# Layer 3 of a four-layer kernel: weighing the gathered rows and the Hadamard transform of z, done in other places

## The chip, the cores and the metric

The kernel runs on one core of one Trainium2 chip. The metric is the device time of one execution in microseconds (us). The runs of the kernel before took 1693.89, 1694.31 and 1697.46 us; the median is 1694.31.

## The reference, cut to what matters

Four layers run behind one another on x, 4 x 512 tokens of 512 channels. Each makes a `ratio` (a scan over time, times a gate of x) and sends it through a feed-forward part. Layer 2 is a mixture of 8 experts with the 2 best taken; its output y is, for each token, the sum of two experts' rows, each times a weight of its own, and is added to x. Layer 3 is the one that the change touches:

```
x = x + y                                       # y: end of layer 2
z = ratio3 * sigmoid(x)
h = fwht(z * SU_ug)                             # Walsh-Hadamard over 512 channels
gate, up = h @ W_gate.T * s_g, h @ W_up.T * s_u # 2048 hidden channels each
hid = silu(gate) * up
x = x + (fwht(hid * SU_dp) @ W_down.T) * s_d
```

A transform over 512 = 4 x 128 channels is a product of a transform over the 4 blocks of 128 channels and one over the 128 channels in each block. The 128-channel part is a matrix (H128) that can be applied to z or, since it is symmetric, to the weights that z is multiplied with. The factors 1/sqrt(n) lie in the scales.

## The kernel before, in words

Channels lie on partitions, tokens along the free dimension. Layer 3 is cut into 4 batches (`BATCH`) of 512 tokens (`TIME`) and 8 chunks (`NCHUNK`) of 256 hidden channels, so 32 units i, chunk by chunk, 4 batches in each. A unit is four products of gate and up (`product`, L2514, 12 matmuls of 512 columns each) and one `down` (L2533, 24 matmuls). Every operand is split into a high part rounded to fp32r and the low rest, and a product is three matmuls: high x high, low x high, high x low. Units 0 to 3 are the first chunk and belong to the start of the layer, in which each batch's z is also made; units 4 to 31 are one steady loop. `gate_up(i)` is followed by `down(i-1)`, so that the work on the hidden channels lies beside TensorE.

For batch i, in order: GpSimd gathers, for each of 4 tiles of 128 tokens, two rows of expert output for each token (`gather`, L1584); VectorE makes diagonal matrices of the weights (`diagonals`, L1592); TensorE turns and weighs with them in one, 32 fp32 matmuls (`cols_of_y`, L1601); `gated` on VectorE adds to x (`residual`, L1647), multiplies with the gate and the ratio (`z`, L1655) and takes the low part (`z_low`, L1660), while ScalarE makes the sigmoid (L1623) and the high part (L1627). Then TensorE transforms all four 128-channel blocks (`fwht`, L1614, 32 matmuls with H128 or its negative), and ScalarE and VectorE split the result again (L1640, L1680). The four blocks of z have one buffer each, `g[0..3]`. `cols_of_y` and `fwht` write the same four PSUM banks as `down`, `p_o`.

The order on each engine is written out by hand (L2445 to L2473 for ScalarE, L2542 to L2575 for TensorE, L2622 to L2647 for VectorE); each engine works through its list in order and waits on semaphores. On the hidden channels ScalarE computes `silu` (L2436) and `high_h` (L2443), VectorE `hidden` (L2593), GpSimd `low_h` (L2487), VectorE `add` (L2603). up of unit i may start when `hidden` of unit i-1 has read the same bank (the event `h0` or `h1`), gate when `silu` has. Weights of a chunk are loaded by SyncE into one buffer `raw`, split by ScalarE (`high`, L2426) and GpSimd (`low`, L2481; chunk 0 by VectorE, `first_low`, L2609), two chunks in turn. Sigmoid and silu live in different ScalarE tables, so going from one to the other costs a table load.

Of the kernel before, what the change touches and what calls it, by code (L numbers as in the profile page):

```python
# [15 lines left out]
P = 128  # L16
# [6 lines left out]
UNITS = CT * BATCH  # L23
FF0, FF1, FF3 = 2048, 1024, 2048
# [1488 lines left out]
class LayerStart:  # L1513
# [3 lines left out]
    def __init__(self, core, scope, d, up_front):  # L1517
# [7 lines left out]
        self.minus_H = sb("in3_minus_H", [P, P], F32R)  # L1525
        self.diag = [[sb(f"in3_diag{k}_{t}", [P, P]) for t in range(TPB)] for k in range(2)]
# [14 lines left out]
class LayerInput:  # L1541
# [4 lines left out]
    def __init__(self, core, scope, c, d, ratio, banks, spare, start):  # L1546
# [7 lines left out]
        self.minus_H, self.su, self.diag = start.minus_H, start.su_ug, start.diag  # L1554
# [31 lines left out]
    def diagonals(self, eng, i):  # L1586
        if i >= 1:
            eng.wait_ge(*self.E("cols_of_y").at(CT * (i - 1) + CT - 1))
        for t in range(TPB):
            for k in range(2):  # L1590
                weight = self.c["moe_weight"][:, i * TPB + t, k:k + 1]
                last = eng.tensor_scalar(self.diag[k][t][:, :], self.c["ident"][:, :], weight, None, ALU.mult)  # L1592
        last.then_inc(*self.E("diag").inc)

    def cols_of_y(self, eng, i):
        eng.wait_ge(*self.E("diag").at(i))
        for t in range(TPB):
            eng.wait_ge(*self.gathered[i % 2 * TPB + t].at(i // 2 * 2 + 1))
            for o in range(CT):
                for k in range(2):  # L1600
                    last = eng.matmul(self.banks[:, o, t * P:(t + 1) * P], self.parts[i % 2][k][t][:, o * P:(o + 1) * P],  # L1601
                                      self.diag[k][t][:, :], start=k == 0, stop=k == 1)
                if t == TPB - 1:
                    last.then_inc(*self.E("cols_of_y").inc)

    def fwht(self, eng, i):
        eng.wait_ge(*self.E("minus_H").at(0))
        eng.wait_ge(*self.E("x").at(CT * i + CT - 1))
        for k in range(CT):
            eng.wait_ge(*self.E("z_low").at(CT * i + k))  # L1610
            for j in range(CT):
                h = self.minus_H if (k & j).bit_count() % 2 else self.c["H128"]
                for t, part in enumerate((self.high(i), self.low(i))):
                    last = eng.matmul(self.banks[:, j, :], h[:, :], part[:, k, :],  # L1614
                                      start=(k + t == 0), stop=(k == CT - 1 and t == 1))
                if k == CT - 1:
                    last.then_inc(*self.E("fwht").inc)
# [7 lines left out]
    def z_high(self, eng, n):  # L1625
        eng.wait_ge(*self.E("z").at(n))
        eng.activation(self.high(n // CT)[:, n % CT, :], self.g[n % CT][:, :], ACT.Copy).then_inc(*self.E("z_high").inc)  # L1627

    def gate_and_round(self, eng, i):
        n = CT * i  # L1630
        self.gate(eng, n)
        for k in range(CT):
            if k + 1 < CT:
                self.gate(eng, n + k + 1)
            self.z_high(eng, n + k)

    def round_transformed(self, eng, i):
        for j in range(CT):
            eng.wait_ge(*self.E("fwht").at(CT * i + j))
            eng.activation(self.high(i)[:, j, :], self.banks[:, j, :], ACT.Copy).then_inc(*self.E("high").inc)  # L1640

    def constants(self, eng):
        eng.tensor_scalar(self.minus_H[:, :], self.c["H128"][:, :].bitcast(F32), -1.0, None, ALU.mult).then_inc(*self.E("minus_H").inc)
# [13 lines left out]
    def z_low(self, eng, n):  # L1657
        k, g = n % CT, self.g[n % CT][:, :]
        eng.wait_ge(*self.E("z_high").at(n))
        eng.tensor_tensor(self.low(n // CT)[:, k, :], g, self.high(n // CT)[:, k, :].bitcast(F32), ALU.subtract).then_inc(*self.E("z_low").inc)  # L1660

    def gated(self, eng, i):
# [6 lines left out]
        self.z_low(eng, n)  # L1669
        self.residual(eng, n + 3)  # L1670
        self.z(eng, n + 2)
        self.z_low(eng, n + 1)
        self.z(eng, n + 3)
        self.z_low(eng, n + 2)
        self.z_low(eng, n + 3)

    def low_transformed(self, eng, i):
        for j in range(CT):
            eng.wait_ge(*self.E("high").at(CT * i + j))
            eng.tensor_tensor(self.low(i)[:, j, :], self.banks[:, j, :], self.high(i)[:, j, :].bitcast(F32), ALU.subtract).then_inc(*self.E("low").inc)  # L1680
# [673 lines left out]
def gated_ffn(core, c, d, ratio, block, before, start):  # L2354
# [10 lines left out]
    w_hi, w_lo = E("weights_hi"), E("weights_lo")  # L2365
    with ExitStack() as s:
# [11 lines left out]
        p_o = core.banks(s, "ffn3_po", [P, CT, TIME])  # L2378
        inp = LayerInput(core, s, c, d, ratio, p_o, (wh[1], wl[1]), start)
# [396 lines left out]
```

## Time and profile before

| | before |
|---|---|
| median of 3 runs | 1694.31 us |
| the profiled execution's own time | 1693.09 us |
| its span | 1691.3 us |
| TensorE busy | 1481.3 us, 88% |
| VectorE busy | 1123.0 us, 66% |
| ScalarE busy | 969.2 us, 57% |
| GpSimd busy | 468.3 us, 28% |
| granted TensorE clock, mean | 0.96 |

The span runs from the first to the last instruction; the execution's own time is a little longer. PE is TensorE (PEld its weight load), DVE VectorE, ACT ScalarE, POOL GpSimd, SP SyncE (SPq its queue). Matmuls are pipelined, so the length of one is longer than the distance between two starts; the distances are what adds up. fp32 matmuls leave two records each, transposes one.

### The profile page before, as it was taken

To read this page: it belongs to the slowest core of one execution; us is meant where nothing else is said; L and a number is where in the kernel's file an instruction comes from. 1 tells how busy PE (TensorE), PEld (TensorE's weight loads), DVE (VectorE), ACT (ScalarE), POOL (GpSimd) and SP (SyncE) were. 2 spreads that over 40 slices of the span, in tenths; PEclk is the share of its full clock that TensorE was granted. 3 is DMA by queue.
4 is the path that set the end of the run, shared out by engine and by line. 5 is a ranking of instruction groups with operands and counts; after the bars stand their busy time and mean duration, and the time that the engine had idled before them with its cause. 6 is when DMAs were issued, how large, how long until landed. Compare 5 with 4: busy or idle time off the path is not lost.

```text
span 1691.3 us, 19555 instructions
## 1 busy us (share of the span) xinstructions
PE 1481.3 (88%) x6389; PEld 959.4 (57%) x6422; DVE 1123.0 (66%) x1718; ACT 969.2 (57%) x1270; POOL 468.3 (28%) x434
## 2 busy tenths in 40 slices
PE   5666579999975699996599999699999999999999
PEld 2222234444432456665544444378788888888887
DVE  6899589999996799995777778754422223222223
ACT  5766499999984799995266877543321221221111
POOL 0000133644431222220044545550231321322211
PEclk9999799999997899999699999899999999999999
DMA  7756642221115898875654545570110100101002
GB/s 279 274 203 209 232 155 76 63 82 63 63 44 152 233 232 211 210 165 193 257 160 148 170 154 168 193 254 1 38 38 1 38 25 14 38 0 38 1 13 88
DMA packets 105495, 210.37 MB, mean 124 GB/s; under 512 B 11508, under 2 KB 28404, under 8 KB 101684
## 3 DMA queue, kind: packets, MB, share of 16 engines
q1 hardware_dynamic: 90500, 173.72, 29.9%
q0 software_dynamic: 14896, 35.40, 9.6%
q8 instruction: 54, 0.88, 0.2%
q14 instruction: 45, 0.37, 0.1%
HBM read 140.13 MB, written 52.17 MB: 114 GB/s over the span
## 4 chain that ended last, share of the span: by engine, by line
PE 49%; DMA 2%; DVE 2%; ACT 1%; issue 0%; POOL 0%; SPq 0%; POOLq 0%; DVEq 0%; ACTq 0%
PE ffn_po L2533 10%; PE ffn_pu L2514 10%; PE ffn_pg L2514 10%; PE moe_psum L1920 8%; PE moe_psum L1941 4%; PE ffn_po L1614 2%; PE ffn_po L1601 1%; PE moe_psum L1859 1%; PE moe_psum L1908 1%; DMA rows_of_z<-moe_zrow 1%; PE moe_psum L1931 0%; DMA in_part<-expert_out,moe_source 0%; DVE x L1647 0%; DVE up_front L1655 0%; DMA rt_consts<-in_route 0%
## 5 line engine op out<-in xcount | busy, mean ns | idle before, releaser
L2593 DVE SCALAR_TENSOR_TENSOR up_front<-ffn_pu,ffn_up_scale,up_front 128x512 f32<-128x512 f32 x64 | 48.0, 751 | 289.9 <-PE ffn_pu L2514 289.9
L2436 ACT ACTIVATE up_front<-ffn_pg,ffn_gate_chunk 128x512 f32<-128x512 f32 x64 | 44.1, 689 | 320.7 <-PE ffn_pg L2514 320.7
L2487 POOL TENSOR_TENSOR ffn_hl<-up_front,ffn_hh 128x512 fp32r<-128x512 f32 x64 | 82.9, 1296 | 396.2 <-ACT ffn_hh L2443 396.2
L2603 DVE SCALAR_TENSOR_TENSOR x<-ffn_po,ffn_out_scale,x 128x512 f32<-128x512 f32 x128 | 95.6, 750 | 75.1 <-PE ffn_po L2533 75.1
L2514 PE MATMUL ffn_pg<-zhi,ffn_wh 128*128 128x512 f32 x256 | 101.5, 397 | 0.5
L2533 PE MATMUL ffn_po<-ffn_hh,ffn_wh 128*128 128x512 f32 x256 | 100.6, 393 | 1.3 <-DVE x L1647 1.3
L2514 PE MATMUL ffn_pu<-zhi,ffn_wh 128*128 128x512 f32 x256 | 100.9, 394 | 0.0
L2514 PE MATMUL ffn_pg<-zhi,ffn_wl 128*128 128x512 f32 x256 | 100.4, 392 | 0.0
L2514 PE MATMUL ffn_pu<-zhi,ffn_wl 128*128 128x512 f32 x256 | 100.4, 392 | 0.0
L2533 PE MATMUL ffn_po<-ffn_hh,ffn_wl 128*128 128x512 f32 x256 | 100.1, 391 | 0.0
L2514 PE MATMUL ffn_pg<-zlo,ffn_wh 128*128 128x512 f32 x256 | 99.6, 389 | 0.0
L2533 PE MATMUL ffn_po<-ffn_hl,ffn_wh 128*128 128x512 f32 x256 | 99.6, 389 | 0.0
L2514 PE MATMUL ffn_pu<-zlo,ffn_wh 128*128 128x512 f32 x256 | 99.3, 388 | 0.0
L965 POOL TENSOR_SCALAR l_rr<-l_ss 128x1 f32<-128x1 f32 x32 | 16.9, 529 | 268.0 <-ACT l_junk L877 203.9
L2443 ACT ACTIVATE ffn_hh<-up_front 128x512 fp32r<-128x512 f32 x64 | 40.2, 628 | 86.5 <-DVE up_front L2593 86.5
L1920 PE MATMUL moe_psum<-up_front,moe_zc 128*128 x156 | 75.1, 605 | 0.0
L1941 PE MATMUL moe_psum<-moe_down,moe_hc 128*128 x156 | 72.2, 593 | 1.9 <-ACT moe_hc L2050 1.9
L1920 PE MATMUL moe_psum<-moe_up_back,moe_zc 128*128 x156 | 73.4, 592 | 0.0
L325 POOL TENSOR_TENSOR wkv_k<-wkv_eu,wkv_k 128x512 f32<-128x512 f32 x32 | 51.9, 1622 | 76.3 <-ACT wkv_eu L315 76.3
L1207 PE MATMUL l_pz<-H_layer,l_gate 128*128 128x512 f32 x128 | 59.8, 611 | 10.6 <-DVE l_gate L1392 10.6
L2132 POOL DMA_INDIRECT moe_zt<-rows_of_z,rt_token_list x39 | 39.9, 1022 | 102.4 <-DVE rt_token_list L2241 80.5
L1234 PE MATMUL l_pg<-H_layer,l_hh 128*128 128x512 f32 x128 | 54.2, 423 | 13.4 <-DVE l_hl L1451 12.9
(354 smaller groups left out, 4053.2 us busy)
## 6 DMA issues: line engine op xcount, KB each, us to landing
wkv_k<-in_fside SPq DMA_DIRECT2D x64, 256.0 KB, 4.3
ratio<-wkv_fn SPq DMA_DIRECT2D x64, 256.0 KB, 3.3
wkv_ek<-exp_k SPq DMA_DIRECT2D x48, 256.0 KB, 3.0
wkv_ekv<-exp_k_times_v SPq DMA_DIRECT2D x48, 256.0 KB, 3.7
expert_out<-moe_eo SPq DMA_DIRECT2D x39, 256.0 KB, 2.2
up_front<-in_gated SPq DMA_DIRECT2D x8, 1024.0 KB, 4.9
x<-in_x SPq DMA_DIRECT2D x4, 1024.0 KB, 7.4
down_first_a<-in_down_raw SPq DMA_DIRECT2D x16, 256.0 KB, 2.6
```

What stands on the lines that cost most here:

```text
L325: eng.tensor_tensor(self.k[p][:, :], self.eu[p][:, :], self.k[p][:, :], ALU.mult).then_inc(*self.E("euv").inc)
L1207: last = eng.matmul(p_z[:, :], z[p][:, k * P:(k + 1) * P], hadamard_row(k).bitcast(F32), start=k == 0, stop=k == CT - 1)
L1234: last = eng.matmul(p_g[:, m * 512:(m + 1) * 512], part[p][:, m * 512 + k * P:m * 512 + (k + 1) * P], hadamard_row(k), start=(k + t == 0), ...
L1920: last = eng.matmul(p_gu[j % 2][:, :], zc[j % ZCS][:, k * P:(k + 1) * P], up[k][:, ds(columns[j], WCOL)], start=k == 0, stop=k == CT - 1)
L1941: last = eng.matmul(p_eo[j % 2][:, :], hc[j % 2][:, k * P:(k + 1) * P], down_w[:, ds(columns[j] + k * EXPERTS * CH, CH)], start=k == 0, st ...
L2436: eng.activation(hf[t], p_g[t][:, :], ACT.Silu, scale=scale).then_inc(*E(f"silu{t}").inc)
L2443: eng.activation(hh[t][slot % 2][:, :], hf[t], ACT.Copy).then_inc(*E(f"hh{t}").inc)
L2487: eng.tensor_tensor(hl[t][slot % 2][:, :], hf[t], hh[t][slot % 2][:, :].bitcast(F32), ALU.subtract).then_inc(*E(f"hl{t}").inc)
L2514: last = eng.matmul(ps[:, :], chunk_w(part, slot, which, k, t), z[:, k, tok], start=(n == 0), stop=(n == 3 * CT - 1))
L2533: last = eng.matmul(p_o[:, o, :], chunk_w(w, slot, "down", k, o), h[k][slot % 2][:, :], start=(n == 0), stop=(n == 3 * HT - 1))
L2593: eng.scalar_tensor_tensor(hf[t], p_u[t][:, :], scale, hf[t], ALU.mult, ALU.mult).then_inc(*E(f"h{t}").inc)
L2603: eng.scalar_tensor_tensor(x[:, o, :], p_o[:, o, :], out_s[:, o:o + 1], x[:, o, :], ALU.mult, ALU.add).then_inc(*E("x").inc)
```

## The change

1. Rows are weighed before they are turned. ScalarE multiplies the first expert's row by its weight (`weigh_first`), VectorE multiplies the second's and adds (`weigh_second`), TensorE only transposes (`cols_of_y`, 16 transposes). `diagonals` and the negative of H128 go. For odd batches the weighed rows lie in the weights' buffer `raw`, so the load of chunk 1 waits until the last batch's rows are turned.
2. The 4-block part of the transform is done by VectorE as butterflies on the four buffers of z: `inner` (blocks 0 and 1, 2 and 3), then `outer` (across the pairs). The blocks are finished in the order 2, 0, 3, 1 (`AS_MADE`), and the products go through them in this order. The high part is taken behind the butterflies, once. `fwht`, `round_transformed` and `low_transformed` go.
3. The 128-channel part is applied to the gate and up weights of each chunk: `turn_weights`, 8 matmuls with H128 in 4 pieces of 512 columns, into the banks of gate and up; ScalarE and VectorE split the result back into the weight buffers (`high_turned`, `low_turned`). For chunks 2 to 7 this stands at the unit with i mod 4 = 2, a unit and a half ahead of use, three pieces in front of `down` and one behind; for chunk 1 between down(2) and down(3), which is moved ahead of gate_up(4); for chunk 0 ahead of everything.
4. The orders on TensorE, ScalarE and VectorE are written anew. In batches 0 to 3 `hidden` stands behind the next-but-one batch's `weigh_second`, and `next_cols` waits for x alone.

Where a function is rewritten, only its new lines are shown; the old ones stand above.

```diff
+AS_MADE = (2, 0, 3, 1)
...
-        self.minus_H = sb("in3_minus_H", [P, P], F32R)
-        self.diag = [[sb(f"in3_diag{k}_{t}", [P, P]) for t in range(TPB)] for k in range(2)]
+        self.spare = sb("in3_spare", [P, TIME])[:, :]
...
+        self.y = [start.parts, [start.raw[:, t * CH:(t + 1) * CH] for t in range(TPB)]]
...
-                eng.wait_ge(*self.E("cols_of_y").at(CT * (i - 2) + CT - 1))
+                eng.wait_ge(*(self.E("y").at(TPB * (i - 2) + t) if i % 2 else self.E("cols_of_y").at(CT * (i - 2) + CT - 1)))
...
+    def weigh_first(self, eng, i, raw_read):
         for t in range(TPB):
             eng.wait_ge(*self.gathered[i % 2 * TPB + t].at(i // 2 * 2 + 1))
+            if i % 2 and t == 0:
+                eng.wait_ge(*(raw_read.at(0) if i == 1 else self.E("cols_of_y").at(CT * (i - 2) + CT - 1)))
+            eng.activation(self.y[i % 2][t], self.parts[i % 2][0][t], ACT.Identity,
+                           scale=self.c["moe_weight"][:, i * TPB + t, 0:1]).then_inc(*self.E("first").inc)
+    def weigh_second(self, eng, i):
+        for t in range(TPB):
+            eng.wait_ge(*self.gathered[i % 2 * TPB + t].at(i // 2 * 2 + 1))
+            eng.wait_ge(*self.E("first").at(i * TPB + t))
+            y, second = self.y[i % 2][t], self.parts[i % 2][1][t]
+            eng.scalar_tensor_tensor(y, second, self.c["moe_weight"][:, i * TPB + t, 1:2], y,
+                                     ALU.mult, ALU.add).then_inc(*self.E("y").inc)
+    def cols_of_y(self, eng, i):
+        for t in range(TPB):
+            eng.wait_ge(*self.E("y").at(i * TPB + t))
             for o in range(CT):
+                last = eng.transpose(self.banks[:, o, t * P:(t + 1) * P], self.y[i % 2][t][:, o * P:(o + 1) * P],
+                                     self.c["ident"][:, :])
                 if t == TPB - 1:
                     last.then_inc(*self.E("cols_of_y").inc)
...
-            eng.wait_ge(*self.E("z_low").at(n - CT))
+            eng.wait_ge(*self.E("z_low").at(n // CT * CT - 1))
...
+    def gates(self, eng, i):
         for k in range(CT):
+            self.gate(eng, CT * i + k)
+    def z_high(self, eng, i):
+        for m, k in enumerate(AS_MADE):
+            eng.wait_ge(*self.E("outer").at(CT * i + m))
+            eng.activation(self.high(i)[:, k, :], self.transformed(k), ACT.Copy).then_inc(*self.E("z_high").inc)
...
+    def inner(self, eng, i, pair):
+        eng.wait_ge(*self.E("z").at(CT * i + 2 * pair + 1))
+        if pair:
+            eng.wait_ge(*self.E("inner").at(CT * i + 1))
+        even, odd = (self.g[2 * pair + k][:, :] for k in range(2))
+        apart = self.g[1] if pair else self.spare
+        eng.tensor_tensor(apart, even, odd, ALU.subtract).then_inc(*self.E("inner").inc)
+        eng.tensor_tensor(even, even, odd, ALU.add).then_inc(*self.E("inner").inc)
+    def transformed(self, k):
+        return self.g[(0, 1, 3, 2)[k]][:, :]
+    def outer(self, eng, i):
+        eng.wait_ge(*self.E("inner").at(CT * i + CT - 1))
+        g = [t[:, :] for t in self.g]
+        eng.tensor_tensor(g[3], g[0], g[2], ALU.subtract).then_inc(*self.E("outer").inc)
+        eng.tensor_tensor(g[0], g[0], g[2], ALU.add).then_inc(*self.E("outer").inc)
+        eng.wait_ge(*self.E("outer").at(CT * i + 1))
+        eng.tensor_tensor(g[2], self.spare, g[1], ALU.subtract).then_inc(*self.E("outer").inc)
+        eng.tensor_tensor(g[1], self.spare, g[1], ALU.add).then_inc(*self.E("outer").inc)
+    def z_low(self, eng, i):
+        for m, k in enumerate(AS_MADE):
+            eng.wait_ge(*self.E("z_high").at(CT * i + m))
+            eng.tensor_tensor(self.low(i)[:, k, :], self.transformed(k), self.high(i)[:, k, :].bitcast(F32),
+                              ALU.subtract).then_inc(*self.E("z_low").inc)
...
         self.residual(eng, n + 2)
         self.z(eng, n + 1)
         self.residual(eng, n + 3)
         self.z(eng, n + 2)
+        self.inner(eng, i, 0)
         self.z(eng, n + 3)
+        self.inner(eng, i, 1)
+        self.outer(eng, i)
+        self.z_low(eng, i)
...
+    PIECES = 2 * GU // TIME
+    turned, turned_hi, turned_lo = E("weights_turned"), E("turned_hi"), E("turned_lo")
...
+        p_w = [p_g[0], p_u[0], p_g[1], p_u[1]]
+        piece = lambda t, n: t[:, n * TIME:(n + 1) * TIME]
...
+                if i == BATCH:
+                    eng.wait_ge(*inp.E("cols_of_y").at(UNITS - 1))
...
+            def high_turned(m):
+                for n in range(PIECES):
+                    eng.wait_ge(*turned.at(PIECES * m + n))
+                    eng.activation(piece(wh[m % 2], n), p_w[n][:, :], ACT.Copy).then_inc(*turned_hi.inc)
...
             high(0, 0)
+            high_turned(0)
+            inp.weigh_first(eng, 0, w_lo)
+            inp.gates(eng, 0)
+            inp.z_high(eng, 0)
+            inp.weigh_first(eng, 1, w_lo)
+            for i in range(1, BATCH):
+                inp.gates(eng, i)
+                for t in range(HT):
+                    silu(i - 1, i - 1, t)
+                inp.z_high(eng, i)
+                if i + 1 < BATCH:
+                    inp.weigh_first(eng, i + 1, w_lo)
+                for t in range(HT):
+                    high_h(i - 1, i - 1, t)
             high(BATCH, BATCH)
+            for i in range(BATCH - 1, N):
                 for t in range(HT):
                     silu(i, i % U, t)
                 for t in range(HT):
                     high_h(i, i % U, t)
+                if i == BATCH - 1:
+                    high_turned(1)
                 if i % BATCH == 1 and i + 3 < N:
                     high(i + 3, (i + 3) % U)
+                if i % BATCH == 2 and i + 2 < N:
+                    high_turned((i + 2) // BATCH)
...
-                eng.wait_ge(*w_lo.at(i // BATCH))
+                eng.wait_ge(*turned_lo.at(PIECES * (i // BATCH) + PIECES - 1))
+                if i % BATCH == 3 and i >= BATCH and i + 1 < N:
+                    eng.wait_ge(*turned_lo.at(PIECES * (i // BATCH + 1) + p_w.index(ps)))
                 if i >= 1:
                     eng.wait_ge(*E(free).at(i - 1))
                 n = 0
-                for k in range(CT):
+                for m, k in enumerate(AS_MADE):
                     if i < BATCH:
-                        eng.wait_ge(*inp.E("low").at(CT * i + k))
+                        eng.wait_ge(*inp.E("z_low").at(CT * i + m))
...
+                eng.wait_ge(*w_lo.at(i // BATCH))
...
+            def turn_weights(m, i, pieces):
+                eng.wait_ge(*w_lo.at(m))
+                for n in pieces:
+                    if i is not None:
+                        eng.wait_ge(*E(("silu", "h")[n % 2] + str(n // 2)).at(i))
+                    for t, part in enumerate((wh, wl)):
+                        last = eng.matmul(p_w[n][:, :], c["H128"][:, :], piece(part[m % 2], n), start=t == 0, stop=t == 1)
+                    last.then_inc(*turned.inc)
             def next_cols(i):
 
+                eng.wait_ge(*inp.E("x").at(CT * i - 1))
                 inp.cols_of_y(eng, i)
 
             before(eng, "zc", "h", "hc", "eo")
+            turn_weights(0, None, range(PIECES))
             inp.cols_of_y(eng, 0)
             product(0, 0, "gate", 0)
+            next_cols(1)
             product(0, 0, "up", 0)
             product(0, 0, "gate", 1)
             product(0, 0, "up", 1)
             product(1, 1, "gate", 0)
+            next_cols(2)
             product(1, 1, "up", 0)
             product(1, 1, "gate", 1)
+            product(1, 1, "up", 1)
             eng.wait_ge(*inp.E("x").at(CT * 2 + CT - 1))
             down(0, 0)
             product(2, 2, "gate", 0)
             product(2, 2, "up", 0)
+            eng.wait_ge(*E("x").at(CT * 0 + CT - 1))
             next_cols(3)
             product(2, 2, "gate", 1)
+            product(2, 2, "up", 1)
             eng.wait_ge(*inp.E("x").at(CT * 3 + CT - 1))
             down(1, 1)
             for i in range(3, N + 1):
                 if i < N:
                     gate_up(i, i % U)
+                m = (i + 2) // BATCH if i % BATCH == 2 and i + 2 < N else None
+                if m is not None:
+                    turn_weights(m, i, range(PIECES - 1))
+                if i != BATCH:
+                    down(i - 1, (i - 1) % U)
+                if m is not None:
+                    turn_weights(m, i, range(PIECES - 1, PIECES))
+                if i == BATCH - 1:
+                    turn_weights(1, i, range(PIECES))
+                    down(i, i)
...
+            def low_turned(m, pieces):
+                for n in pieces:
+                    eng.wait_ge(*turned_hi.at(PIECES * m + n))
+                    eng.tensor_tensor(piece(wl[m % 2], n), p_w[n][:, :], piece(wh[m % 2], n).bitcast(F32),
+                                      ALU.subtract).then_inc(*turned_lo.inc)
             first_low()
+            low_turned(0, range(PIECES))
+            inp.weigh_second(eng, 0)
             inp.gated(eng, 0)
+            inp.weigh_second(eng, 1)
+            for i in range(1, BATCH):
+                inp.gated(eng, i)
+                if i >= 2:
+                    add(i - 2, i - 2)
+                if i + 1 < BATCH:
+                    inp.weigh_second(eng, i + 1)
+                for t in range(HT):
+                    hidden(i - 1, i - 1, t)
+            for i in range(BATCH - 1, N + 1):
                 if i < N:
                     if i % BATCH == 0:
                         chunk_scale(i, i % U)
                     for t in range(HT):
                         hidden(i, i % U, t)
+                m = (i + 2) // BATCH if i % BATCH == 2 and i + 2 < N else None
+                if m is not None:
+                    low_turned(m, range(PIECES - 1))
+                if i != BATCH:
+                    add(i - 1, (i - 1) % U)
+                if m is not None:
+                    low_turned(m, range(PIECES - 1, PIECES))
+                if i == BATCH - 1:
+                    low_turned(1, range(PIECES))
+                    add(i, i)
```

## Rows read from the trace of the kernel before

**Rows 1.** The chain of waits, 1087 to 1225 us: start us, length us, what
```profile
1103.84 9.24 PE ffn_po L1614 x32
...
1118.93 7.14 PE ffn_po L1601 x64
...
1131.59 7.44 PE ffn_po L1614 x32
...
1203.88 3.00 PE ffn_pg L2514 x12
1206.88 2.75 PE ffn_pu L2514 x12
...
1215.12 5.49 PE ffn_po L2533 x24
```

**Rows 2.** The same chain later: in the steady loop, and its last piece
```profile
1253.60 2.76 PE ffn_pg L2514 x12
...
1676.93 10.94 PE ffn_po L2533 x48
```

**Rows 3.** Busy time of each engine by stretch: a batch, then the steady loop
```profile
1178.00:1210.00 32.00, 31.23 (x165) 26.08 (x164) 14.07 (x23) 14.81 (x19) 5.34 (x3) 1.00 0.00 1
...
1309.00:1440.00 131.00, 131.00 (x574) 107.36 (x573) 35.81 (x50) 25.55 (x34) 34.45 (x18) 1.00 0.07 25
```

**Rows 4.** TensorE's timeline: four transposes in the experts and what follows
```profile
1060.52 0.60 PE L1908 MATMUL moe_psum<-ident,moe_zt 128*128 128x128 f32 x4
1060.96 1.88 PE L1920 MATMUL moe_psum<-up_front,moe_zc 128*128 x4
```

**Rows 5.** VectorE's timeline: first weight split, batch 0's first instructions
```profile
1087.62 3.37 DVE L2609 TENSOR_TENSOR ffn_wl<-up_front,ffn_wh 128x3072 fp32r<-128x3072 f32 x1
...
1099.06 1.28 DVE L1647 TENSOR_TENSOR x<-x,ffn_po 128x512 f32<-128x512 f32 x2 [8.07 <-PE ffn_po L1601]
1100.53 0.75 DVE L1655 SCALAR_TENSOR_TENSOR up_front<-up_front,in_su,zhi 128x512 f32<-128x512 f32 x1 [0.18 <-ACT up_front L1623]
1101.19 0.68 DVE L1647 TENSOR_TENSOR x<-x,ffn_po 128x512 f32<-128x512 f32 x1
1101.79 0.74 DVE L1655 SCALAR_TENSOR_TENSOR up_front<-up_front,in_su,zhi 128x512 f32<-128x512 f32 x1
1102.45 0.68 DVE L1660 TENSOR_TENSOR zlo<-up_front,zhi 128x512 fp32r<-128x512 f32 x1
```

**Rows 6.** ScalarE's timeline: four copies, a rounding, a table load
```profile
1111.72 2.07 ACT L1640 ACTIVATE zhi<-ffn_po 128x512 fp32r<-128x512 f32 x4 [5.40 <-PE ffn_po L1614]
...
1119.76 0.63 ACT L2443 ACTIVATE ffn_hh<-up_front 128x512 fp32r<-128x512 f32 x1 [2.85 <-DVE up_front L2593]
1120.41 1.28 ACT L1623 ACT_TABLE_LOAD   x1
```

**Rows 7.** TensorE's timeline behind idle time (in brackets), earlier layer first
```profile
576.52 0.50 PE L1234 MATMUL l_pg<-H_layer,l_hh 128*128 128x512 f32 x1 [2.85 <-DVE l_hl L1451]
576.86 0.40 PE L1234 MATMUL l_pg<-H_layer,l_hl 128*128 128x512 f32 x1
...
1103.84 0.58 PE L1614 MATMUL ffn_po<-zhi,H 128*128 128x512 f32 x1 [3.47 <-DVE x L1647]
1104.21 0.63 PE L1614 MATMUL ffn_po<-zlo,H 128*128 128x512 f32 x1
1104.64 0.63 PE L1614 MATMUL ffn_po<-zhi,H 128*128 128x512 f32 x1
```

**Rows 8.** SyncE's queue, then DMA issues of 1080 to 1141 with landing time
```profile
1098.34 0.37 SPq L1576 DMA_DIRECT2D zhi<-ratio  x1
...
up_front<-down_full SPq DMA_DIRECT2D x1, 512.0 KB, 9.2
```

**Rows 9.** VectorE's timeline: four adds of down's result
```profile
1160.21 2.72 DVE L2603 SCALAR_TENSOR_TENSOR x<-ffn_po,ffn_out_scale,x 128x512 f32<-128x512 f32 x4
```

**Rows 10.** GpSimd's timeline: low parts of hidden channels, of a weight chunk
```profile
1136.58 2.57 POOL L2487 TENSOR_TENSOR ffn_hl<-up_front,ffn_hh 128x512 fp32r<-128x512 f32 x2
...
1252.30 6.85 POOL L2481 TENSOR_TENSOR ffn_wl<-up_front,ffn_wh 128x3072 fp32r<-128x3072 f32 x1 [1.36 <-ACT ffn_wh L2426]
```

**Rows 11.** Timelines of GpSimd, then VectorE, in the experts' last steps
```profile
1079.94 1.63 POOL L369 TENSOR_TENSOR wkv_fn<-wkv_fn,wkv_bn 128x512 f32<-128x512 f32 x1 [1.76 <-DVE wkv_bn L355]
...
1080.48 1.63 DVE L513 SCALAR_TENSOR_TENSOR wkv_fd<-wkv_fd,wkv_eu 128x512 f32<-128x512 f32 x1
...
1083.68 0.69 DVE L513 SCALAR_TENSOR_TENSOR wkv_fd<-wkv_fd,wkv_eu 128x512 f32<-128x512 f32 x1
```

More of the change, by code:

```diff
@@ L1553, in __init__ @@
         self.e = {}
-        self.minus_H, self.su, self.diag = start.minus_H, start.su_ug, start.diag
+        self.su, self.spare = start.su_ug, start.spare
         own = [start.parts, [core.sb(scope, f"in3_part{t}", [P, CH], F32)[:, :] for t in range(TPB)]]
@@ L1584, in gather @@
                 eng.indirect_dma_start(self.parts[i % 2][k][t], None, self.d["expert_out"], at).then_inc(*self.gathered[i % 2 * TPB + t].inc)
[L1586 to L1593, printed above, removed]
@@ L1599, in cols_of_y @@
             for o in range(CT):
-                for k in range(2):
-                    last = eng.matmul(self.banks[:, o, t * P:(t + 1) * P], self.parts[i % 2][k][t][:, o * P:(o + 1) * P],
-                                      self.diag[k][t][:, :], start=k == 0, stop=k == 1)
+                last = eng.transpose(self.banks[:, o, t * P:(t + 1) * P], self.y[i % 2][t][:, o * P:(o + 1) * P],
+                                     self.c["ident"][:, :])
                 if t == TPB - 1:
                     last.then_inc(*self.E("cols_of_y").inc)
-    def fwht(self, eng, i):
-        eng.wait_ge(*self.E("minus_H").at(0))
-        eng.wait_ge(*self.E("x").at(CT * i + CT - 1))
-        for k in range(CT):
[L1610 to L1617, printed above, removed]
@@ L1668, in gated @@
         self.z(eng, n + 1)
-        self.z_low(eng, n)
         self.residual(eng, n + 3)
         self.z(eng, n + 2)
-        self.z_low(eng, n + 1)
+        self.inner(eng, i, 0)
         self.z(eng, n + 3)
[L1674 to L1680, printed above, removed]
+        self.inner(eng, i, 1)
+        self.outer(eng, i)
+        self.z_low(eng, i)
 def experts(core, c, d, ratio, ratio3, up_front, up_in, block, start):
@@ L2572, in _ @@
                     gate_up(i, i % U)
-                if i == 3:
-                    eng.wait_ge(*inp.E("low").at(UNITS - 1))
-                down(i - 1, (i - 1) % U)
+                m = (i + 2) // BATCH if i % BATCH == 2 and i + 2 < N else None
[8 more added lines that the diff above has]
+                    down(i, i)
         @block.vector
         def _(eng):
-            inp.constants(eng)
             eng.wait_ge(*consts.at(3))
@@ L2620, in _ @@
             chunk_scale(0, 0)
+            def low_turned(m, pieces):
[3 more added lines that the diff above has]
+                                      ALU.subtract).then_inc(*turned_lo.inc)
             first_low()
+            low_turned(0, range(PIECES))
+            inp.weigh_second(eng, 0)
             inp.gated(eng, 0)
-            inp.diagonals(eng, 1)
-            inp.low_transformed(eng, 0)
-            hidden(0, 0, 0)
-            inp.gated(eng, 1)
-            inp.diagonals(eng, 2)
-            hidden(0, 0, 1)
-            inp.low_transformed(eng, 1)
-            hidden(1, 1, 0)
-            inp.gated(eng, 2)
-            inp.diagonals(eng, 3)
-            add(0, 0)
-            hidden(1, 1, 1)
-            inp.low_transformed(eng, 2)
-            hidden(2, 2, 0)
-            inp.gated(eng, 3)
-            add(1, 1)
-            hidden(2, 2, 1)
-            inp.low_transformed(eng, 3)
-            for i in range(3, N + 1):
+            inp.weigh_second(eng, 1)
[8 more added lines that the diff above has]
+            for i in range(BATCH - 1, N + 1):
                 if i < N:
@@ L2646, in _ @@
                         hidden(i, i % U, t)
-                add(i - 1, (i - 1) % U)
+                m = (i + 2) // BATCH if i % BATCH == 2 and i + 2 < N else None
[8 more added lines that the diff above has]
+                    add(i, i)
 def build(nc, d, out):
```

55 lines of the change are left out of this document (removed).

## The prediction, on record before the changed kernel ran

> **What bounds the kernel now.** I read the chain of waits first. From 1087 us on it is TensorE nearly alone [rows 1]: gathered rows turned and weighed (L1601), the transform of z (L1614), the products (L2514, L2533). The last product ends at 1676.93 + 10.94 = 1687.87 us [rows 2]. Then the engines' busy time by stretch [rows 3]: over one batch of the start of layer 3 (1178 to 1210) TensorE is busy 31.2 of 32 us, VectorE 14.1, ScalarE 14.8; in the long stretch behind, TensorE is busy all the time and VectorE 27% of it. So a TensorE instruction removed from this layer shortens the end by its whole length, until VectorE or ScalarE becomes late in its place. The reader should keep two prices: 12 products take 2.75 us, so 0.229 us each; 32 transform matmuls take 7.44 us, so 0.2325 each [rows 1].
>
> **The sum of TensorE's work.** Removed: `fwht`, 32 matmuls a batch, 7.44 us in batches 1 to 3 and 9.24 in batch 0, where the clock starts low [rows 1]. `cols_of_y` takes 7.14 us a batch with 32 fp32 matmuls (64 records) [rows 1]; after the change it is 16 transposes. Four transposes of the same shape in the experts take 1060.96 - 1060.52 = 0.44 us [rows 4], so 16 take 1.8 us: 5.3 us less a batch. Added: `turn_weights`, 8 matmuls of the transform's form for each of 8 weight chunks, 1.86 us a chunk. Alone this would give, from batch 1 on, 3 x (7.44 + 5.3) - 7 x 1.86 = 38.3 - 13.0 = 25.3 us. But the transform's other half is now on VectorE, and the batches' start must be walked through.
>
> **The unit of the walk: `gated` on VectorE.** Its instructions start 0.60 us (tensor_tensor) or 0.66 us (scalar_tensor_tensor) behind one another [rows 5]: `x` at 1101.19, `z` at 1101.79, next at 1102.45. Before, its z part took 12 instructions a batch, plus 4 for the rounding of the transformed. Now it is 20: 4 residuals, 4 z, 8 sums and differences, 4 roundings. The first z starts 1.47 us behind the first residual, since ScalarE's sigmoid lies between (1099.06 to 1100.53) [rows 5]. From there: the last z at +5.88; the second inner pair waits until that z has landed, +6.69; `outer` waits likewise, +8.03, and for its own first two, +9.36; the four roundings at +10.57 to +12.4. ScalarE's four copies lie one step ahead (0.52 us apart [rows 6]). Sum: **13.05 us from the first residual to the end of `gated`**, and a product can begin at +11.25, when the first rounded bank is there. With 0.1 us less or more at each of five same-engine waits I bound it at 12.5 and 13.6.
>
> **Batch 0: nothing gained.** The 8 `in_diag` instructions ahead of `first_low` go (1.7 us); it ended at 1087.62 + 3.37 = 1090.99 [rows 5] and now ends near 1089.3. Turning chunk 0 costs 8 matmuls at the low clock, 0.43 us each [rows 7], then copies and differences: done by 1094.1. All of this is covered, because the last of the first gathers lands only at 1098.3, when the queue that waits for it issues its next load [rows 8]; if that cover went, it would cost 4 us at most. Behind the landing now stand a ScalarE pass (0.63), a VectorE pass (0.75) and a transpose at low clock (0.6 with latency): first residual at 1100.35, against 1099.06. `gated` ends at 1113.4. The product waits idle for 11 us, and the clock falls: behind 3.47 us of idleness the matmuls are 0.43 us apart [rows 7]. Eight at 0.43 and four at 0.23 from 1111.65 on end at 1116.0. Before, the same product ended at 1116.2 (1113.19 + 3.0). Even.
>
> **Batch 1.** `weigh_second` (4 x 0.66) ends at 1116.1, transposes start at 1116.0, first residual at 1117.65, `gated` ends at T1 = 1130.7.
>
> **Batch 2.** VectorE: `weigh_second` +2.65, two `hidden` to +4.0. ScalarE: `high_h` 0.63, then a table load of 1.28 [rows 6], then the sigmoid; the first z starts at T1 + 6.7, 1.1 us later than VectorE alone would. T2 = T1 + 18.3 = 1149.0. TensorE has 8.25 + 5.5 us to do in it beside its 2.75: covered.
>
> **Batch 3.** Here a new wait decides. TensorE's order is product(2, gate), product(2, up), then `next_cols(3)`, and the up product needs h0 of unit 1, that is `hidden(1,0)`, which on VectorE stands behind `gated(2)`, `add(0)` (4 x 0.68 [rows 9]) and `weigh_second(3)`: T2 + 2.75 + 2.65 + 0.75 = T2 + 6.15. The gate product ends at T2 + 1.6, TensorE is idle for 4.5 us, and by the row of 3.47 us the clock falls; a gap of 2.85 us left it up [rows 7]. The up product takes 4.35 us instead of 2.75, transposes 1.8: first residual at T2 + 12.0 = 1161.0, T3 = 1174.05.
>
> **Unit 3 and on.** The gate product ends at T3 + 0.9; product(3, up, 0) needs `hidden(2,0)` behind `add(1)`: T3 + 3.5, 2.6 us idle. gate_up(3) ends at 1177.55 + 8.25 = 1185.8. Before it ended at 1215.12 [rows 1]. **Gain up to here 29.3 us.** Then down(2) to 1191.3. Turning chunk 1 needs `low(4)`: the weights are issued behind the last `cols_of_y` (1161.3) and land 9.2 us later at the worst [rows 8], ScalarE copies them at 1179 to 1182, GpSimd's 6.85 us [rows 10] end by 1189: in time. From gate_up(4) on the work is as before, plus 7 turns: 56 x 0.2325 = 13.0 us. The six turns of later chunks need GpSimd's low part one unit earlier than now: it ends at 1252.30 + 6.85 = 1259.15 [rows 10], and gate_up(6) of the same stretch ends at 1264.6 (from 1253.60, 11.0 us on): 5.4 us to spare. The turned pieces' copies (0.52 and 0.62 us each) lie beside down (5.49 us) and, the fourth, beside the next 8 us of products. `chunk_scale` and SyncE's loads get no new neighbour that waits long. I take these bubbles as 0; bounds 0 and 7 x 1.6 = 11 us (a copy and a difference seen in full at every turn, with the last matmul).
>
> **The forecast.** 29.3 - 13.0 = 16.3 us. The profiled execution took 1693.09 us for a span of 1691.3; it becomes 1676.8. The median of the runs shown, 1694.31, stands 1.2 us above it, and becomes **1678.0 us**. The own range of this case is 1671.5 to 1686: the walk's three `gated` by 0.5 each, the clock in the 4.5 us gap (1.6), small turn bubbles.
>
> **Rivals.**
> *TensorE stays the bound.* VectorE keeps up because the waits of h0 overlap better than I walked. For it: TensorE was busy 98% of such a batch [rows 3]. Against: 20 + 4 + 2 + 4 VectorE instructions of 0.6 to 0.68 us make about 19.5 us a batch where TensorE has 18.3. It gives the 25.3 us of the sum plus the 1.9 us that TensorE idled before: 1667 to 1669. Chance 0.12.
> *The turns show.* Copies and differences of each turn are not hidden, 11 us of 16: 1683 to 1690, with GpSimd's low part late as the worst of it. Against it: 5.4 us to spare at each. Chance 0.12.
> *VectorE's two-operand passes slow down beside GpSimd (slower than before).* The change puts 16 such instructions with both operands in SBUF in a batch where 8 stood, and 4 more to weigh. In the experts' stage one and the same instruction (L513) takes 0.69 us once, and 1.63 us beside a GpSimd tensor_tensor of 1.63 us [rows 11]. If that extra 0.94 us falls on most of the 80 instructions, it costs up to 75 us: 1700 to 1750. It decides from 16.3 / 80 = 0.2 us each, or 17 of them hit in full. Against it: in these batches GpSimd computes only 2 x 1.29 us a batch [rows 10], most of it while VectorE adds from PSUM. Chance 0.04. The Trainium skill ("SBUF — State Buffer", Who interferes with whom) states that a VectorE instruction with two SBUF inputs contends with a GpSimd instruction that reads SBUF; the two lengths of L513 agree with it, and by that rule 2.6 us a batch at most could be lost here, 10 us in all, which would leave the kernel 6 us faster.
> The forecast itself has 0.70. The last 0.02 is for no change: the gain eaten by something that I don't see.
>
> **Chances and range.** No change means within 0.2% (3.4 us), about what this measurement can tell. Faster: 0.70 + 0.12 + 0.12 less a little of the turns' upper end, 0.94; same 0.02; slower 0.04. The range 1668 to 1687 leaves out the slow rival, the top of the turns' case and a little below.
>
> **What would show it.** In the changed profile: no L1614 group on TensorE, 64 matmuls with H and the weights; `cols_of_y` in 1.8 us; gate_up(3) ending near 1186; TensorE idle about 11 us ahead of the first product, 4.5 us ahead of product(2, up, 0), 2.6 ahead of product(3, up, 0), all ended by VectorE's `hidden` or roundings; a 13.05 us `gated`. It is wrong if `gated` is over 14 us, if a turn is followed by idleness on TensorE, or if the matmul distance in the long stretch isn't 0.229 us.

## The result, and the profile after

The changed kernel takes 1680.85 us (median of 1682.31, 1681.88, 1679.81, 1676.61), the kernel before beside it 1694.1 us: ratio 0.991, interval 0.9892 to 0.9927. Foretold were 1678.0 us and 1668 to 1687.

The layers ahead, which the change leaves alone, do not always end at the same time: in the profiled executions the experts' last matmul ends at 1077.90 us before and at 1080.10 us after, and in the traces of the experiments anywhere from 1075.31 to 1084.33 us. From here on I count from that matmul's end to the end of the layer's last (1687.87 and 1677.32 us): **609.97 us before, 597.22 after, 12.75 less, where 16.3 were forecast.** That stretch splits at the first `residual` of each batch on VectorE ("to batch 1" runs from batch 0's first `residual` to batch 1's):

| us | to batch 0 | to batch 1 | to batch 2 | to batch 3 | to the end | sum |
|---|---|---|---|---|---|---|
| before | 21.16 | 25.72 | 25.96 | 32.38 | 504.75 | 609.97 |
| forecast | 22.45 | 17.3 | 17.05 | 26.3 | 510.6 | 593.7 |
| after | 22.96 | 18.46 | 17.42 | 26.98 | 511.40 | 597.22 |

The chain of waits of the changed kernel, batches 0, 2 and 3, which answers to [rows 1]:

```profile
1102.55 0.49 PE ffn_po L1607
...
1114.39 5.46 PE ffn_pg L2524 x12
1119.85 1.65 PE ffn_po L1607 x13
...
1152.94 2.77 PE ffn_pg L2524 x12
1155.71 3.11 issue
1158.82 5.46 PE ffn_pu L2524 x12
1164.28 1.93 PE ffn_po L1607 x16
...
1177.26 3.00 PE ffn_pg L2524 x12
1180.26 2.05 issue
1182.31 2.99 PE ffn_pu L2524 x12
...
1188.05 2.75 PE ffn_pu L2524 x12
```

L1614 is gone, `cols_of_y` (now L1607) takes 1.9 us or less, and TensorE stands still where it was said to: ahead of product(2, up, 0) for 3.1 us and of product(3, up, 0) for 2.05, and, ahead of the first product, for 10.7 us. The trace puts the first two down to "issue"; that they are waits for `hidden` follows from VectorE's timeline. The first of the two `hidden` below ends near 1158.7 us, and TensorE starts at 1158.82; the next ones begin at 1181.47, the first ends near 1182.2, and TensorE starts at 1182.31.

```profile
1157.98 1.40 DVE L2615 SCALAR_TENSOR_TENSOR up_front<-ffn_pu,ffn_up_scale,up_front 128x512 f32<-128x512 f32 x2
```

The timeline of VectorE in batch 0 (answers to [rows 5]):

```profile
1103.06 1.28 DVE L1629 TENSOR_TENSOR x<-x,ffn_po 128x512 f32<-128x512 f32 x2 [0.57 <-PE ffn_po L1607]
...
1113.56 2.58 DVE L1663 TENSOR_TENSOR zlo<-up_front,zhi 128x512 fp32r<-128x512 f32 x4
1116.06 2.73 DVE L1600 SCALAR_TENSOR_TENSOR up_front<-ffn_wl,moe_weight,up_front 128x512 f32<-128x512 f32 x4
```

`gated` lasts 1113.56 + 2.58 - 1103.06 = 13.08 us; 13.05 were worked out. Busy times, batch 3's start and the steady loop (answers to [rows 3]; TensorE is no longer full in the first, the clock's mean is 0.86):

```profile
1155.00:1180.00 25.00, 21.82 (x92) 17.25 (x90) 18.18 (x29) 10.07 (x14) 2.51 (x2) 0.86 0.18 63
1300.00:1400.00 100.00, 100.00 (x436) 81.78 (x435) 30.34 (x43) 21.96 (x33) 26.97 (x14) 1.00 0.09 32
```

The steady loop's chain, one turn (1311.41 is the `down` behind three turned pieces), two products at the same place of two chunks, the last piece ([rows 2]):

```profile
1311.41 5.45 PE ffn_po L2544 x24
1317.33 2.80 PE ffn_pg L2524 x12
...
1385.30 2.80 PE ffn_pg L2524 x12
...
1666.38 10.94 PE ffn_po L2544 x48
```

A chunk takes 1385.30 - 1317.33 = 67.97 us; without a turn it is 4 x 16.49 = 65.96 (16.49 from one `down` to the next: 1328.90 - 1312.41 of e4, below). A turn costs 2.01 us where 1.86 stood in the sum: nothing of copies and differences shows, but the four products behind a turn take 2.80 instead of 2.75 us each. The first of the seven turns, chunk 1's, takes 1.86 us, as worked out.

### The profile page after: what moved, and what is told of

The parts are those of the page before. It is cut to its first block, busy times and chain, and to the rows that moved or that the text cites. A ratio compares the mean times of both kernels' runs of the same rounds, so it can differ in the third digit from the quotient of the medians.

```text
span 1680.5 us, 19164 instructions
## 1 busy us (share of the span) xinstructions
PE 1454.7 (87%) x6133; PEld 930.0 (55%) x6166; DVE 1157.3 (69%) x1749; ACT 985.4 (59%) x1300; POOL 467.6 (28%) x434
## 4 chain that ended last, share of the span: by engine, by line
PE 47%; DVE 3%; DMA 1%; issue 1%; POOL 1%; ACT 1%; SPq 0%; POOLq 0%; DVEq 0%; ACTq 0%
PE ffn_pg L2524 11%; PE ffn_po L2544 10%; PE ffn_pu L2524 10%; PE moe_psum L1919 8%; PE moe_psum L1940 4%; PE moe_psum L1858 1%; PE moe_psum L1907 1%; PE moe_psum L1930 0%; POOL up_front L1585 0%; PE ffn_pu L2555 0%; PE ffn_pg L2555 0%; PE ffn_po L1607 0%; DVE up_front L1637 0%; DVE rt_hot_block L2212 0%; DMA rt_consts<-in_route 0%
## 5 line engine op out<-in xcount | busy, mean ns | idle before, releaser
L2524 PE MATMUL ffn_pg<-zhi,ffn_wh 128*128 128x512 f32 x256 | 102.9, 402 | 13.6 <-DVE zlo L1663 13.6
```

The source lines that it names most:

```text
L2524: last = eng.matmul(ps[:, :], chunk_w(part, slot, which, k, t), z[:, k, tok], start=(n == 0), stop=(n == 3 * CT - 1))
```

## The experiments

All times in the table of the experiments are counted as above, in each one's own profile; the ratio is that of the whole times to the kernel before run beside it. The kernel before had medians of 1696.31 us beside e1 to e4, 1696.48 beside e5 to e8 and 1701.57 beside e9 to e12, which ran on three different chips; so medians of different groups can't be set side by side, ratios can. A stretch is that of one execution each. The intervals of the ratios of e3 and e6 overlap that of the change (0.9892 to 0.9927), and those of e5 and e8 touch it, so what they gain over it rests on the traces.

| | to 0 | to 1 | to 2 | to 3 | to end | sum | median, ratio [interval] |
|---|---|---|---|---|---|---|---|
| e1 weighing alone | 23.65 | 21.69 | 25.43 | 30.19 | 507.04 | 608.00 | 1689.47, 0.9952 [0.9934, 0.9969] |
| e2 diagonals back | 26.52 | 22.65 | 20.80 | 27.04 | 511.57 | 608.58 | 1693.37, 0.9984 [0.9962, 1.0005] |
| e3 cols 3 first | 23.22 | 18.07 | 17.37 | 20.37 | 512.77 | 591.80 | 1677.86, 0.9884 [0.9846, 0.9921] |
| e4 no turns | 23.24 | 18.05 | 17.37 | 24.51 | 501.15 | 584.32 | 1671.59, 0.9854 [0.9816, 0.9892] |
| e5 hidden first | 22.95 | 18.21 | 19.43 | 20.97 | 509.10 | 590.66 | 1673.87, 0.986 [0.9822, 0.9898] |
| e6 warm | 23.12 | 17.40 | 17.37 | 27.10 | 511.43 | 596.42 | 1678.91, 0.9901 [0.9868, 0.9934] |
| e7 no butterflies | 23.25 | 12.23 | 14.37 | 22.24 | 508.82 | 580.91 | 1663.59, 0.9802 [0.9764, 0.984] |
| e8 hidden first, warm | 23.11 | 17.39 | 19.41 | 20.97 | 509.09 | 589.97 | 1673.25, 0.9862 [0.9826, 0.9898] |
| e9 order, warm | 23.35 | 31.06 | 17.37 | 20.36 | 511.07 | 603.21 | 1685.93, 0.9903 [0.9882, 0.9924] |
| e10 after again | 23.16 | 29.90 | 18.48 | 25.07 | 511.40 | 608.01 | 1688.0, 0.991 [0.989, 0.9929] |
| e11 before again | 29.75 | 26.56 | 26.25 | 32.34 | 504.75 | 619.65 | 1706.1, one run |
| e12 hidden first from 2 | 23.24 | 29.90 | 18.63 | 21.14 | 509.10 | 602.01 | 1683.13, 0.9877 [0.984, 0.9913] |

**e1, the first part alone, in the kernel before.** `cols_of_y` and `gather` are those of the change; ScalarE's and VectorE's passes stand where I put them:

```diff
-            inp.diagonals(eng, 2)
+            inp.weigh_second(eng, 2)
...
             inp.gate_and_round(eng, 1)
+            inp.weigh_first(eng, 2, w_lo)
```

> The kernel before with the first part of the change alone: rows weighed by ScalarE and VectorE, 16 transposes for 32 fp32 matmuls; z's transform stays on TensorE. If TensorE bounds the start of the layer throughout (theory), each of batches 1 to 3 gives 7.14 - 1.8 = 5.3 us, batch 0 loses 1 to 2 us because two more passes stand behind its last gather: 14 us less than before, about 1680. Rival: weigh_second delays the rounding of the transformed z on VectorE and TensorE waits for it; then under 8 us, 1686 or more.

The theory's 14 us is refuted: 2.0 us in the stretch, 8 by the ratio (5 to 11 by its interval). The rival, under 8 us, fits the trace and lies at its edge by the ratio. (The two lie 6 us apart; what the unprofiled executions did differently no trace shows.) The chain of e1 between batches 1 and 2 runs through `weigh_first` (2.55 us), a table load, `silu`, `hidden` and only then the rounding of the transformed z; TensorE's 5.3 us a batch turn into waiting, and one product and two `down`s take longer than at the high clock (4.27 us, and 7.36 and 7.42 where they took 5.75 and 5.73 before). So this is the value of part 1 in this order, not its best.

**e2, the first part undone.** `diagonals` and the old `cols_of_y` in place of `weigh_first`, `weigh_second` and the transposes, the diagonals in `raw`.

> The changed kernel with its first part undone: diagonal matrices and 32 fp32 matmuls again, the diagonals held in the weight buffer. Theory (the start is a loop through VectorE, in which the turned rows of batch i are a link): first residual 4.3 us later in batch 1, about 1.6 in batch 2, 4.3 in batch 3, 1.5 sooner in batch 0: 8 to 9 us slower than the changed kernel, about 1689. Rival (TensorE has room in the start, so its 5.3 us a batch hide): 0 to 3 us slower.

Slower by 11.4 us in the stretch. Batch 1 as expected (+4.2), batch 2 by more (+3.4, where I had 1.6), batch 3 not at all; batch 0 is 3.6 us later where I had it sooner, since the 32 fp32 matmuls now start behind the turning and the differences, partly at the low clock. Either part alone leaves 1.4 or 2.0 us of gain in the stretch; both give 12.75. By the ratios it is 3 us (no gain at all lies within its interval) and 8 us, and 15 together, which points the same way but would not show it by itself.

**e3, one wait moved.**

```diff
             product(2, 2, "gate", 0)
-            product(2, 2, "up", 0)
             eng.wait_ge(*E("x").at(CT * 0 + CT - 1))
             next_cols(3)
+            product(2, 2, "up", 0)
```

> The changed kernel with next_cols(3) ahead of product(2, up, 0), as in batches 1 and 2. Theory: the up product's wait for hidden(1,0) and the low clock behind it hold up batch 3; its first residual comes 6.5 us sooner (behind weigh_second, 0.5 us for the last transposes), TensorE no longer falls to the low clock there: 6 to 6.5 us less than the changed kernel, 1674 to 1675. Rival: the wait only moves, to product(3, up, 0) behind add(1); then 0 to 3 us less.

5.4 us less in the stretch. The interval to batch 3 is 6.6 shorter, as worked out; 1.4 come back behind it, because TensorE now has the up product in front of its last work. The rival falls, but for a part: product(3, up, 0) still waits 1.49 us.

**e4, no turns for chunks 2 to 7** (the computation leaves out this part of the transform).

> The changed kernel without the turning of the gate and up weights of chunks 2 to 7 (48 matmuls, 24 copies, 24 differences left out; these chunks use the weights as loaded). Theory (copies and differences hidden, no bubbles): 6 x 1.86 = 11.2 us less than the changed kernel, about 1669.5. Rival (each turn also shows a copy and a difference): 18 to 22 us less, 1659 to 1663.

12.9 us less in the stretch; 2.5 of them are in the interval to batch 3, which has no turn in it (product(2, up, 0) ran at the high clock there), and its product(3, up, 0) took 4.43 us for 2.99. What is left is 11.8, about 6 turns at 2.0. The chain in the steady loop, and TensorE's timeline at the two products, with the gaps ahead of them:

```profile
1312.41 2.76 PE ffn_pg L2522 x12
...
1328.90 2.76 PE ffn_pg L2522 x12
```

```profile
1158.61 0.47 PE L2522 MATMUL ffn_pu<-zhi,ffn_wh 128*128 128x512 f32 x1 [3.26 <-DVE up_front L2613]
...
1179.62 0.47 PE L2522 MATMUL ffn_pu<-zhi,ffn_wh 128*128 128x512 f32 x1 [2.21 <-DVE up_front L2613]
```

**e5, `hidden` first on VectorE.**

```diff
                 inp.gated(eng, i)
+                for t in range(HT):
+                    hidden(i - 1, i - 1, t)
                 if i >= 2:
                     add(i - 2, i - 2)
                 if i + 1 < BATCH:
                     inp.weigh_second(eng, i + 1)
-                for t in range(HT):
-                    hidden(i - 1, i - 1, t)
```

> The changed kernel with hidden(i-1) directly behind gated(i) on VectorE, ahead of add and weigh_second. Theory: product(2, up, 0) and product(3, up, 0) no longer wait (3.1 and 2.05 us of idleness, 2.7 us of low clock), the first residual of batch 3 comes about 6.2 us sooner and gate_up(3) ends 9 us sooner: about 9 us less than the changed kernel, 1672. Rival: the add and weigh_second pushed back by 1.4 us delay the turned rows as much as is gained; then 0 to 3 us less.

6.6 us less, not 9. Both waits are gone, but the interval to batch 2 is 2.0 us longer (19.43 for 17.42). The timelines of VectorE and GpSimd in e5, then VectorE's of the changed kernel, show why:

```profile
1133.35 4.78 DVE L1600 SCALAR_TENSOR_TENSOR up_front<-in_part,moe_weight,up_front 128x512 f32<-128x512 f32 x4
```

```profile
1133.52 3.39 POOL L2495 TENSOR_TENSOR ffn_hl<-up_front,ffn_hh 128x512 fp32r<-128x512 f32 x2 [3.60 <-ACT ffn_hh L2453]
```

```profile
1134.47 2.73 DVE L1600 SCALAR_TENSOR_TENSOR up_front<-in_part,moe_weight,up_front 128x512 f32<-128x512 f32 x4
```

The same four instructions take 4.78 us beside GpSimd's `low_h` and 2.73 beside none, and `low_h` 3.39 for 2.57 [rows 10]. In e1 one `z_low` takes 2.09 us for 0.68 beside the same GpSimd instruction. The rule of the Trainium skill that the prediction cited ("SBUF — State Buffer", Who interferes with whom) agrees with both.

**e6, TensorE kept busy ahead of the first product.**

```diff
             inp.cols_of_y(eng, 0)
+            eng.wait_ge(*turned_lo.at(PIECES - 1))
+            for n in range(28):
+                eng.matmul(p_u[1][:, :], c["H128"][:, :], piece(wh[0], n % PIECES), start=True, stop=True)
```

> The changed kernel with 28 idle matmuls of H128 with the weights into a free bank between cols_of_y(0) and product(0, gate, 0), so that TensorE isn't idle for 10.7 us there. Theory: the first product then runs at the high clock, ends 3 us sooner, and batch 1's first residual comes 2.4 us sooner, since weigh_second(1) is late next: 2 to 2.5 us less than the changed kernel. Rival: the idle matmuls last past the first rounded bank, or the clock falls later in the start again, and nothing is gained: within 1 us.

0.8 us less, which one execution can't tell from chance; the rows say what became of the 2.4. The clock rose during the 28, which so took 7.8 us and left 3.27 us of idleness. The first product's timeline shows that the price of a gap can come later than its end: five matmuls 0.23 us apart, then 0.43.

```profile
1113.73 0.47 PE L2524 MATMUL ffn_pg<-zhi,ffn_wh 128*128 128x512 f32 x1 [3.27 <-DVE zlo L1663]
1114.04 0.40 PE L2524 MATMUL ffn_pg<-zlo,ffn_wh 128*128 128x512 f32 x1
...
1115.19 0.62 PE L2524 MATMUL ffn_pg<-zhi,ffn_wh 128*128 128x512 f32 x1
1115.61 0.63 PE L2524 MATMUL ffn_pg<-zlo,ffn_wh 128*128 128x512 f32 x1
```

**e7, no butterflies** (the 4-block part of the transform is left out): `inner` and `outer` are not called, `z_high` waits for z.

> The changed kernel without the 8 sums and differences of each batch (z goes through rounding as made; the 4-block part of the transform is left out). Theory (VectorE's gated bounds batches 0, 1 and 3; TensorE is next in batch 2): 5.1 us less in each of these three, 13 to 15 us less than the changed kernel, about 1667. Rival (TensorE bounds the start as before the change): 0 to 3 us less.

16.3 us less, 6.2, 3.1 and 4.7 of them in the intervals to batches 1, 2 and 3 and 2.6 behind; 13 to 15 were expected. VectorE's `gated` bounds the start; with TensorE as the bound this would have been 0 to 3.

**e8, e5 and e6 together.**

> The orders of e5 and the idle matmuls of e6 together in the changed kernel. Theory: the gains add, since they lie in different batches: 11 us less than the changed kernel, about 1670. Rival: the gain of e6 is taken up by TensorE's work in batch 2, which is then late: as e5 alone.

7.25 us less than the changed kernel, 0.7 less than e5: they add, as far as 0.7 us can tell, but e6 has little to give.

**e9, the order of e3, `hidden(2)` ahead of `add(1)`, 40 idle matmuls.**

> The changed kernel with next_cols(3) ahead of product(2, up, 0), hidden(2) ahead of add(1) in batch 3 alone, and 40 idle matmuls ahead of product(0, gate, 0). In e5 weigh_second(2) took 4.78 us beside GpSimd's low_h, against 2.73 in the changed kernel; this order keeps the two apart. Theory, counted from the experts' last matmul to this layer's last: 5.4 us as in e3, 1.7 for the wait of product(3, up, 0), 2.4 for the first product at the high clock: 9.5 us less than the changed kernel. Rival: the last two gains hide behind one another or behind weigh_second(1), as in e8; then 7 us less, no better than e8.

**e10 and e11, both kernels once more.**

> The changed kernel unchanged, to see how far one and the same kernel differs from execution to execution. Theory: the stretch from the experts' last matmul to this layer's last repeats within 1.5 us (the phase of the clock in two cold products), near 597.2 us; what differs by more lies in the layers ahead. Rival: the stretch itself differs by 3 us or more.

> The kernel before, unchanged. Theory: the same stretch is near 610.0 us again, within 1 us, so that the change gives 12 to 13.5 us in it. Rival: it differs by 3 us or more, and the 12.8 us between the two traces is partly chance.

Both expectations fell and their rivals hold, because of a stall that the other ten traces don't have: 11 to 14 us ahead of batch 1 in e9, e10 and e12, and 8.6 ahead of batch 0 in e11. TensorE's and VectorE's timelines in e10:

```profile
1121.41 0.39 PE L2524 MATMUL ffn_pg<-zhi,ffn_wh 128*128 128x512 f32 x1
1122.58 0.40 PE L2524 MATMUL ffn_pg<-zlo,ffn_wh 128*128 128x512 f32 x1 [0.78 <-issue]
1124.68 0.39 PE L2524 MATMUL ffn_pg<-zhi,ffn_wl 128*128 128x512 f32 x1 [1.70 <-issue]
```

```profile
1129.66 1.28 DVE L1629 TENSOR_TENSOR x<-x,ffn_po 128x512 f32<-128x512 f32 x2 [14.17 <-remote]
```

Matmuls whose operands are ready come 2 us apart, and VectorE waits for what the trace cannot name, while the gathers go on. In e11 TensorE's matmuls come without such gaps and end at 1105.2, and only VectorE stands still, until 1111.10; whether that is the same stall is not shown. The four traces with a stall are all those of e9 to e12, which ran on one chip, and of e1 to e8, on two others, none has it; the medians of both kernels are higher in e9 to e12 too (1701.57 and 1688.0 us), in the same ratio as at first, 0.991; so what lengthens them strikes both kernels about alike. Whether the chip is the reason is not shown, and the cause of the stall stays open. Behind the stall the last column repeats to 0.01 us (e11 and before, e10 and after); between, single intervals move by 1 to 2 us (25.07 for 26.98) with TensorE's clock.

Because of it, e9 can only be judged behind batch 1: 548.8 us, against 555.0 in e10 and 555.8 in the changed kernel without the stall, so 6.2 or 7.0 less; e5 and e8 gained 6.3 over the latter. (e10 and the changed kernel are the same program; the clock makes the difference.) e3 has the same order but for `hidden(2)` ahead of `add(1)`, and from batch 2's first `residual` on e9 is 1.7 us shorter (531.4 against 533.1), just what that wait was to give. So the rival isn't borne out for this term; what the 40 matmuls give is covered by the stall and not shown.

**e12, e5 with batch 1's order as in the change.**

> As e5, but in batch 1 weigh_second(2) stands ahead of hidden(0) again, as in the changed kernel, so that it isn't beside GpSimd's low_h. Theory (the shared access to SBUF cost e5 its missing 2 us): weigh_second(2) back to 2.7 us, batch 2's first residual back at 58.8 us from the experts' last matmul instead of 60.6, and the stretch 1.5 to 2 us shorter than e5's 590.7. Rival (e5's order itself cost it, not the overlap): the stretch stays within 0.5 us of e5's or is longer.

`weigh_second(2)` is back at 2.73 us, so the overlap with `low_h` was what lengthened it in e5. Whether the kernel gains by it is not settled. Behind batch 1 e12 gains 6.1 us over e10, where e5 gained 6.3 over the changed kernel: by these sums nothing. But TensorE was held up by something else in e12. Behind the stall it was idle for 5.79 us ahead of batch 1's first product, whose transposes then began 5.25 us behind its start (e5: 4.43), and batch 2's first `residual` waited for them:

```profile
1147.08 1.29 DVE L1629 TENSOR_TENSOR x<-x,ffn_po 128x512 f32<-128x512 f32 x2 [1.67 <-PE ffn_po L1607]
```

From that product's start to the end of gate_up(3) e12 takes 51.01 us and e5 51.63, although e12 lost 0.8 us more to the low clock in that product alone. So neither the theory nor its rival falls.

## Why the prediction was right

The mechanism was: VectorE's `gated` sets the pace of the start, the turns are hidden, TensorE waits for `hidden` at two places. Each of these shows in the rows; what was off were sizes, above all that of the clock.

**Batch 0 even, its cover.** Turning chunk 0 was hidden as said. The first residual came 0.5 us late; the last gather landed at 1100.9 less the 2.2 us shift, 1098.7 for 1098.3.

**`gated` as the unit.** Right to 0.03 us, and e7 shows that it is what counts.

**The clock behind the gaps.** The mis-sized term. I let eight matmuls run at the low clock, 0.43 us apart, and four at 0.23 (4.4 us). All twelve of the first product ran at the low one (5.46 us, 1114.39; the granted clock is 0.50 from 1115 to 1120), which is 1.1 us, and again in product(2, up, 0) (5.46 for 4.35, 1158.82), 1.1 more. The clock also fell behind the start of the first product of batch 1, where I had counted no loss (4.59 us for 2.75). That cost nothing on balance: batch 2's first `residual` came 0.4 us late, but its first z stands as I put it, 6.7 us behind the end of `gated`, since it waits for ScalarE:

```profile
1141.24 0.75 DVE L1637 SCALAR_TENSOR_TENSOR up_front<-up_front,in_su,zhi 128x512 f32<-128x512 f32 x1 [1.02 <-ACT up_front L1616]
```

TensorE's lateness then came off its idle time ahead of product(2, up, 0), 3.1 us for 4.5. In e4 and e10 that same product took 3.0 us (behind a gap of 3.26) and 4.57 us (behind 2.29), so this term moves by 2.5 us between executions.

**The waits for `hidden`.** Right in place, and shorter than said: 3.1 us for 4.5 and 2.05 for 2.6 (e5 removes both). It was worth more to remove them than to have foreseen them.

**The turns.** Hidden as said (e4). The six in the steady loop take 2.01 us for 1.86, and all seven together cost 13.8 us for 13.0, 0.8 more.

Together: 0.5 us in batch 0, 1.1 in the first product, 1.1 in product(2, up, 0) (in the table 0.4 to batch 2 and 0.7 to batch 3) and 0.8 for the turns give the 3.5 us between 16.3 and 12.75.

That the median came within 3 us of 1678.0 is partly luck. The profiled execution took 1682.31 us where 1676.8 were worked out, 5.5 more: 3.5 from the stretch and 2.2 from the layers ahead, less 0.2 behind the last matmul. I then put the median 1.2 us above the profiled execution, and it came 1.5 below, which gave 2.7 back.

**The rivals.** TensorE as the bound: refuted by e7, by TensorE's idle time in the changed kernel (10.7, 2.8, 3.1 and 2.05 us), and by e2, whose three intervals are 13.6 us shorter than before where its TensorE has three `fwht` of 7.44 us less to do. Turns that show: refuted by e4. The two-operand passes beside GpSimd: the mechanism is real (e1, e5), but in the changed kernel `low_h` falls on residuals, which read PSUM, and nothing is lost. The sum of TensorE's work alone, 25.3 us, is twice what was gained: 21.2 us are won in the three intervals, and 1.8 and 6.65 given back at both ends.

The best version for the stretch without the stall is e8, 20.0 us under the kernel before; it is 0.9862 of it, the changed kernel 0.991 beside its own.

## What to carry to other kernels

When work goes from a full engine to two others, walk the loop through all of them: two changes that each free the full engine can be worth less alone than together (2.0 and 1.4 us in the traces against 12.75, 8 and 3 by the ratios against 15). Look up what each engine has in front of the small instruction that another waits for; here swapping two lines was worth 6.6 us in the trace, half as much as the whole change. Before moving a two-operand VectorE pass, see what GpSimd does at that time.

## What was not expected of the hardware

A gap of 3.27 us left the clock high for five matmuls and took it down then (e6), and one of 2.83 us did likewise behind three matmuls in the changed kernel (its first product of batch 1); by the rows of before I had taken a gap as either harmless or paid at once [rows 7]. Nor does the length of the gap alone set its price: 3.26 us cost nothing (e4, 3.01 us for the product behind it), while 2.21 us in the same trace and 2.29 us in e10 brought products of 4.43 and 4.57 us. And the unexplained stall of 8.6 to 14 us, in both kernels, at different places.
